# A Flamingo-style block on one core: new step orders in cross- and local attention, layer norms on ScalarE, roots taken in pairs, the queries' root inside the exponential

## What is computed

```python
def local_layer(x, wqkv, qs, ksc, wo, lg, lb, w1, b1, w2, b2):
    h = shift_token(x)
    q, k, v = split_heads(h @ wqkv)           # 8 heads of 64
    q, k = l2norm(q) * qs, l2norm(k) * ksc
    q, k = rotary_xpos(q, k)
    o = local_attention(q, k, v)              # windows of 64, each sees itself and the one before; softmax
    x = x + merge(o) @ wo
    h = layernorm(shift_token(x)) * lg + lb
    a, g = split(h @ w1 + b1)
    return x + (a * gelu(g)) @ w2 + b2

x = x + tanh(g_xattn[0]) * cross_attention_0(layernorm(x), ctx)   # 16 heads of 8, causal and padding mask
y = layernorm(x)
for l in range(2):
    y = local_layer(y, ...)
x = x + tanh(g_ffn[0]) * y
x = x + tanh(g_xattn[1]) * cross_attention_1(layernorm(x), ctx)   # with biases, padding mask
x = x + tanh(g_ffn[1]) * experts(layernorm(x))                    # 8 experts, the top two of a sigmoid router
```

## Time and profile before

| | |
|---|---|
| median of the runs | 1339.03 us |
| the profiled execution | 1336.5 us, its span 1334.6 us |
| mean granted TensorE clock | 0.969 |
| busy: TensorE, VectorE, ScalarE, GpSimd | 1147.0, 1070.7, 875.5, 876.7 us (86%, 80%, 66%, 66%) |
| chain that ended last | VectorE 33%, TensorE 25%, ScalarE 19%, issue 14%, GpSimd 6% |

### The profile page before, as it was taken

The page is one execution under the profiler, slowest core; times in us unless marked ns, Lnnn a source line. Parts: engine busy times, 40 slices in busy tenths (PEclk is TensorE's granted clock), DMA queues, the critical chain, the costliest instruction groups (busy, mean ns, idle before and its releaser), DMA issues.

```text
span 1334.6 us, 33990 instructions
## 1 busy us (share of the span) xinstructions
PE 1147.0 (86%) x11792; PEld 963.0 (72%) x11792; DVE 1070.7 (80%) x2430; ACT 875.5 (66%) x2445; POOL 876.7 (66%) x1060
## 2 busy tenths in 40 slices
PE   5487776689999997896899999979979999999997
PEld 3266654477777776895677777769966777899997
DVE  2799997788888884777888888858889998588887
ACT  1376664477877775454777777765557777666664
POOL 0567773999999993336999999953366664334442
PEclk8699998899999998997999999999989999999999
DMA  6100000000000000210011100001100000000000
GB/s 171 51 8 4 1 1 7 8 8 10 10 10 10 14 2 9 62 31 11 10 24 41 28 10 15 2 4 29 28 1 2 1 2 1 5 14 13 13 11 15
DMA packets 59418, 23.35 MB, mean 17 GB/s; under 512 B 49093, under 2 KB 57202, under 8 KB 59250
## 3 DMA queue, kind: packets, MB, share of 16 engines
q1 hardware_dynamic: 55296, 19.22, 6.0%
q10 hardware_dynamic: 3954, 1.96, 0.6%
HBM read 10.68 MB, written 2.10 MB: 10 GB/s over the span
## 4 chain that ended last, share of the span: by engine, by line
DVE 33%; PE 25%; ACT 19%; issue 14%; POOL 6%; ACTq 1%; DMA 1%; SPq 1%; DVEq 0%; POOLq 0%
ACT a_e L889 12%; PE m_ps_h L1232 7%; PE m_ps_y L1244 6%; DVE a_rot L994 6%; DVE x_e L626 6%; DVE x_stat L623 5%; DVE a_rot L996 3%; DVE a_stat L952 3%; ACT a_sq L896 2%; PE a_ps_t L804 2%; ACT x_qhh L532 2%; DVE a_stat L945 2%; PE f_ps_y L1089 1%; PE f_ps_g L1100 1%; POOL a_stat L1020 1%
## 5 line engine op out<-in xcount | busy, mean ns | idle before, releaser
L1020 POOL TENSOR_TENSOR a_stat<-a_stat,small 128x16 f32<-128x16 f32 x64 | 187.7, 2933 | 5.3
L889 ACT ACTIVATE a_e<-a_ps_s,a_stat 128x128 f32<-128x128 f32 x512 | 180.2, 379 | 4.4 <-DVE a_stat L952 3.5
L1030 POOL TENSOR_TENSOR a_e<-a_e,a_stat 128x1024 f32<-128x1024 f32 x64 | 121.4, 1896 | 19.6 <-DVE a_stat L981 19.6
L1024 POOL TENSOR_TENSOR a_rot<-a_rot,a_stat 128x1024 f32<-128x1024 f32 x64 | 121.8, 1903 | 5.0
L518 ACT ACTIVATE x_e<-x_e 128x1024 f32<-128x1024 f32 x64 | 67.8, 1060 | 69.9 <-DVE x_e L626 69.9
L889 ACT ACTIVATION_READ_ACCUMULATOR a_e<-a_ps_s,a_stat 128x1 f32 x512 | 111.4, 218 | 0.0
L994 DVE TENSOR_TENSOR a_rot<-a_ps_qk,a_rtab 128x512 f32<-128x512 f32 x128 | 87.9, 686 | 26.9 <-ACT a_sq L896 26.8
L882 ACT ACTIVATE a_eT<-a_ps_t 128x1024 f32<-128x1024 f32 x64 | 65.6, 1024 | 61.9 <-PE a_ps_t L804 59.3
L1130 ACT ACTIVATE f_gl<-f_ps_g,vec 128x128 f32<-128x128 f32 (+1 forms) x192 | 55.9, 361 | 64.1 <-PE f_ps_g L1100 64.1
L1016 POOL TENSOR_TENSOR a_rot<-a_rot 128x512 f32<-128x512 f32 x64 | 82.1, 1283 | 23.0 <-DVE a_rot L996 20.9
L1232 PE MATMUL m_ps_h<-m_hT,w 128*128 128x128 f32 x768 | 93.6, 278 | 0.0
(11 more groups left out here) (165 smaller groups left out, 3659.7 us busy)
## 6 DMA issues: line engine op xcount, KB each, us to landing
a_h<-y SPq DMA_DIRECT2D x64, 32.0 KB
f_h<-y SPq DMA_DIRECT2D x64, 32.0 KB
out_dram<-x SPq DMA_DIRECT2D x32, 64.0 KB, 1.5
a_h<-y SPq DMA_DIRECT2D x64, 31.8 KB
f_h<-y SPq DMA_DIRECT2D x64, 31.8 KB
wqkv<-in_L_ffn_wqkv_dram SPq DMA_DIRECT2D x2, 768.0 KB, 4.9
w<-in_L_ffn_w_dram SPq DMA_DIRECT2D x2, 768.0 KB, 5.5
c_ctx2T<-in_ctxT_dram SPq DMA_DIRECT2D x2, 512.0 KB, 3.2
```

The source lines that it names most:

```text
L889: act.activation(self.e[n % 2][:, P * i:P * i + P], ps_s[:, P * i:P * i + P], ACT.Exp, bias=stat[:, i:i + 1], accum_out=stat[:, 8 + i:9 + ...
L1020: p.tensor_tensor(t[:, 48:64], t[:, 32:48], g.neg_half.broadcast_to([P, 16]), ALU.pow).then_inc(self.s_n, 1)
L1024: p.tensor_tensor(r, r, t[:, 48:64].unsqueeze(2).broadcast_to([P, 16, LD]), ALU.mult).then_inc(self.s_n, 1)
L1030: p.tensor_tensor(e3, e3, self.stat[n % 2][:, 16:24].unsqueeze(2).broadcast_to([P, 8, P]), ALU.mult)\
```

## The change

- **Local attention, the roots.** Keys are still multiplied by their root on GpSimd (512 columns); the queries are not. Their root goes in as the `scale` of the exponential, and the maximum is multiplied by it on VectorE (8 columns). The mask is smaller in size (-1e24) for that. The statistics have four buffers where they had two.
- **Local attention, the order.** All engines have new sequences with lower depths. TensorE: transposes of e (s-6), v (s-4), h (s), o (s-6), transposes of q and k (s-2), qk (s, k first), y (s-6), scores (s-3). ScalarE: square q (s-1), kTr (s-3), copies of v (s-4, half of it to `vx` in each tile), eT (s-6), hT (s), exponentials (s-4), square k (s). The rounding of the weights (ScalarE) and the position tables (VectorE) move to step -3, the rest of the rounding to step -2, the loads to two steps earlier.
- **Cross-attention, the norms.** The `Norm` helper is no longer used. The statistics of the norm before the attention and (in cross 0) of the norm behind it, eight tiles earlier (`LAG`), are put side by side; GpSimd adds, takes one power of both and computes -mean * root (`roots`). ScalarE applies scale and bias for h and for y.
- **Cross-attention, the order.** New sequences and lower depths on all engines; on VectorE: subtraction (s-4), reciprocal (s-6), update of x (s-7), division (s-6), statistics (s), in cross 0 statistics for y (s-7), maximum (s-3), rest of the queries' rounding (s-2). The spread of the keys is divided between the two steps of a pair.
- **Starts.** 0, 36, 69, 106, 139, 174 and 209, and the steps begin at -3.

The core of the diff:

```diff
@@ Cross.scalar
+        n = s - 1
+        if 0 <= n < T:
+            k, t = T * l + n, self.st[n % 4]
+            act.wait_ge(self.s_rs, self.rooted(l, n))
+            after(act, self.s_h, k - 1)
+            act.activation(self.h[n % 2][:, :], tok(g.x, n), ACT.Identity, bias=t[:, 20:21], scale=t[:, 18:19]).then_inc(self.s_hn, 1)
+        m = n - LAG
+        if not l and 0 <= m < T:
+            t = self.st[n % 4]
+            act.wait_ge(self.s_rs, self.rooted(0, n))
+            act.activation(tok(g.y, m), tok(g.x, m), ACT.Identity, bias=t[:, 21:22], scale=t[:, 19:20]).then_inc(self.s_yn, 1)
@@ Cross.roots
+        p.tensor_scalar(t[:, 16 + lo:16 + hi], both[:, lo:hi, 1], 1e-5, None, ALU.add).then_inc(self.s_rs, 1)
+        p.wait_ge(self.s_rs, k + 1)
+        p.tensor_tensor(t[:, 18 + lo:18 + hi], t[:, 16 + lo:16 + hi], self.g.neg_half.broadcast_to([P, hi - lo]), ALU.pow)\
+            .then_inc(self.s_rs, 1)
+        p.wait_ge(self.s_rs, k + 2)
+        for i in range(lo, hi):
+            m = p.tensor_scalar(t[:, 20 + i:21 + i], t[:, 12 + 2 * i:13 + 2 * i], t[:, 18 + i:19 + i], -1.0, ALU.mult, ALU.mult)
@@ Local.tensor
+        n = s - 6
+        if 0 <= n < T:
+            k = T * l + n
+            pe.wait_ge(self.s_en, k + 1)
+            pe.wait_ge(self.s_qc, min(k + 4, end))
+            pe.wait_ge(self.s_kc, min(k + 4, end))
+            for i in range(2 * LP):
+                m = pe.transpose(ps_t[:, P * i:P * i + P], self.e[n % 2][:, P * i:P * i + P], g.ident)
+            m.then_inc(self.s_et, 1)
+        n = s - 4
+        if 0 <= n < T:
+            k = T * l + n
+            after(pe, self.s_vc, k)
+            after(pe, self.s_oc, k - 2)
+            self.project_h(pe, ps_b[:, :], n, 1024).then_inc(self.s_v, 1)
+        n = s
+        if 0 <= n < T:
...
+            pe.transpose(ps_a[:, 0:P], self.h[n % UNROLL][:, :], g.ident).then_inc(self.s_h, 1)
+        n = s - 6
+        if 0 <= n < T:
+            k, u, b = T * l + n, n % 2, n // 2
+            pe.wait_ge(self.s_ec, k + 1)
+            if u:
+                pe.wait_ge(self.s_vx[0], k // 2 + 1)
+                pe.wait_ge(self.s_vx[1], k // 2 + 1)
+            pe.wait_ge(self.s_vc, min(k + 3, end))
...
+                        m = pe.matmul(ps_b[LD * e:LD * e + LD, P * pair + WIN * x:P * pair + WIN * x + WIN],
@@ Local.scalar
+        n = s - 4
+        if 0 <= n < T:
+            k, u, b = T * l + n, n % 2, n // 2
+            rows = slice(0, WIN) if u else slice(WIN, P)
+            act.wait_ge(self.s_v, k + 1)
+            after(act, self.s_o, k - 2)
+            act.activation(self.vx[b % 2][rows, :], ps_b[rows, :], ACT.Copy).then_inc(self.s_vx[u], 1)
+            act.activation(self.vt[n % UNROLL][:, :], ps_b[:, :], ACT.Copy).then_inc(self.s_vc, 1)
+        n = s - 6
+        if 0 <= n < T:
+            k = T * l + n
+            act.wait_ge(self.s_et, k + 1)
+            after(act, self.s_o, k - 1)
+            act.activation(self.eT[n % 2][:, :], ps_t[:, :], ACT.Copy).then_inc(self.s_ec, 1)
...
+            for i in range(2 * LP):
+                e, pair = divmod(i, LP)
+                root = 48 + 2 * pair + e
+                act.activation(self.e[n % 2][:, P * i:P * i + P], ps_s[:, P * i:P * i + P], ACT.Exp, bias=stat[:, 24 + i:25 + i],
+                               scale=stat[:, root:root + 1], accum_out=stat[:, 8 + i:9 + i]).then_inc(self.s_e, 1)
@@ Local.gpsimd
+            r = self.rot[n % 2][:, INNER:].rearrange("p (h d) -> p h d", d=LD)
+            p.tensor_tensor(r, r, t[:, 56:64].unsqueeze(2).broadcast_to([P, LH, LD]), ALU.mult).then_inc(self.s_n, 1)
@@ build
-        for stage, l, later in ((cross, 0, 0), (local, 0, T + 4), (mlp, 0, T + 2), (local, 1, T + 4), (mlp, 1, T + 2),
-                                (cross, 1, T + 3), (experts, 0, T + 5)):
+        for stage, l, later in ((cross, 0, 0), (local, 0, T + 4), (mlp, 0, T + 1), (local, 1, T + 5), (mlp, 1, T + 1),
+                                (cross, 1, T + 3), (experts, 0, T + 3)):
```

More of the change, by code:

```diff
@@ L479, in tensor @@
             m.then_inc(self.s_s, 1)
-        n = s - 8
+        n = s - 2
+        if 0 <= n < T:
+            k = T * l + n
+            pe.wait_ge(self.s_hc, k + 1)
+            after(pe, self.s_qc, k)
+            after(pe, self.s_qr, k)
+            if n == 0 and l:
+                self.take(pe, l, "q")
+            for i in range(2):
+                m = pe.matmul(ps_q[:, P * i:P * i + P], g.wq[l][:, P * i:P * i + P], self.hT[n % 2][:, :], start=True, stop=True)
+            m.then_inc(self.s_q, 1)
+        n = s - 6
         if 0 <= n < T:
@@ L726, in sync @@
     def sync(self, sp, l, s):
-        if s == 0 and not l:
+        if s == -2 and not l:
             sp.wait_ge(self.s_z, 2)
-        n = s
+        n = s + 2
         if 0 <= n < T:
@@ new lines, in tensor @@
+        n = s - 2
+        if 0 <= n < T:
+            k = T * l + n
+            pe.wait_ge(self.s_n, 4 * k + 4)
+            pe.wait_ge(self.s_nq, k + 1)
+            after(pe, self.s_ec, k - 3)
+            after(pe, self.s_qc, k)
+            after(pe, self.s_kc, k)
+            if n == 0:
+                self.take(pe, l, "t")
+            for i in range(2 * LP):
+                m = pe.transpose(ps_t[:, P * i:P * i + P], self.rot[n % 2][:, P * i:P * i + P], g.ident)
+            m.then_inc(self.s_t, 1)
@@ new lines, in tensor @@
+        n = s
+        if 0 <= n < T:
+            k = T * l + n
+            pe.wait_ge(self.s_hc, k + 1)
+            pe.wait_ge(self.s_hr, k + 1)
+            if n == 0:
+                self.take(pe, l, "qk")
+            for i in range(2):
+                lo = INNER * (1 - i)
+                after(pe, self.s_sq, 2 * (k - 1) + i + 1)
+                after(pe, self.s_r, 4 * (k - 1) + 2 * i + 2)
+                self.project_h(pe, ps_qk[:, lo:lo + INNER], n, lo).then_inc(self.s_qk, 1)
+        n = s - 6
@@ new lines, in tensor @@
+        if 0 <= n < T:
+            k = T * l + n
+            pe.wait_ge(self.s_oc, k + 1)
+            after(pe, self.s_yc, k)
+            pe.wait_ge(self.s_hc, min(k + 7, end))
+            pe.wait_ge(self.s_hr, min(k + 7, end))
+            for pair in range(LP):
+                m = pe.matmul(ps_a[:, 0:D], self.oT[n % 2][:, P * pair:P * pair + P], g.lwo[:, D * pair:D * pair + D],
+                              start=(pair == 0), stop=(pair == LP - 1))
+            m.then_inc(self.s_y, 1)
```

517 lines of the change are left out of this document (229 added, 288 removed).

## The result

The changed kernel takes 1423.57 us (median of four runs, 1422.02 to 1425.22) against 1338.82 for the kernel before, a ratio of 1.063 [1.0616, 1.0645]. The forecast was 1371 with 1345 to 1405 as its range: the sign was right, 84.7 us were lost where 32.5 had been expected, and the time lies outside the range. The profiled execution has a span of 1420.8 us against 1334.6, so 86.2 us have to be found.

A forecast was written before the change was run, and what follows sets the result against it. GpSimd was taken to bound local attention, VectorE the first cross-attention, TensorE nearly the second. 1336.5 + 68 (local) - 20 - 6 (cross) - 9.5 (seams) = 1369.0, with 2.5 for the median 1371.5, stated as 1371 us; range 1345 to 1405.

The forecast's parts named there:

- one chain through TensorE and ScalarE: Local attention: transposes of e, v, ScalarE's copies, o, then TensorE's remaining groups in order, 9.8 us a step.
- some 2.1: Local attention: microseconds of each step in which TensorE stands empty, waiting in front of o for ScalarE's copies.
- 29 x 9.8 + 2 x 7.8: Local layer, 31 steps from tile 0's maximum to tile 31's: 299.8 us against 265.7, so +34 us.
- a rival at 0.08: Local attention: TensorE's clock falls, one step in ten at the lower clock, 37 us more, 1408 us; chance 0.08.
- 68 for both layers: Local attention: loss of 34 us in each of two layers, +68 us together, bounds +50 to +91.
- The seams: Passages between stages: -9.5 us together, bounds +5 to -22.
- I take 7 off: Seam between first cross-attention and first local maximum: 7 us less than its 33.7 us, with weight rounding moved earlier.
- -20: First cross-attention: 20 us gained as both norms leave VectorE for ScalarE, bounds 0 to -30.
- -6: Second cross-attention: 6 us gained as VectorE saves 9 us and TensorE caps it, bounds +3 to -12.
- why the step is no shorter: Local attention before: GpSimd's queue, 8.50 us from root to root without a gap that matters, sets the 8.57 us step.
- My rival of a faster kernel at 1262: Local attention: the detour through ScalarE doesn't bind, steps of about 7.9 us, each layer 21 us less; chance 0.09.
- 62 x 0.72 = 45 us: Local attention: the exponentials' second per-partition operand on ScalarE, 0.72 us a step, 45 us without cover, costed at nothing.

The follow-up runs named there:

- e1: Changed kernel with local v projection (tile s-3) moved to the end of TensorE's step, behind the scores: 1343.68 us, ratio 1.0024.
- e3: Changed kernel with 14 unused transposes of the identity in TensorE's queue ahead of h in local attention: 1401.76 us, ratio 1.0463.
- e9: Changed kernel with v last, scores a step later between transposes of e and h, padding row last, maximum ahead of k's rotation: 1385.47 us, ratio 1.0334.
- e7: Changed kernel with the rounding of weights and the position tables back at step 0 of both local stages: 1429.5 us, ratio 1.0687.
- e4: Kernel before with the changed kernel's cross-attention alone, experts two steps earlier, local attention as before: 1315.02 us, ratio 0.9812.
- e12: e5 with the changed kernel's early rounding (steps -3 and -2) in both local stages: 1303.29 us, ratio 0.9726.
- e2: Changed kernel with ScalarE's copy of e's transposes ahead of its two copies of v: 1360.52 us, ratio 1.0149.
- e5: e4 with ScalarE's copy of the padding row moved to the end of its cross-attention step: 1306.2 us, ratio 0.9766.
- e8: e4 with the queries' root moved from GpSimd into the exponential's scale, the maximum multiplied on VectorE: 1366.42 us, ratio 1.0204.
- e11: e8 without the exponentials' per-partition scale and with the unmultiplied maximum as bias: 1316.47 us, ratio 0.9822.
- e10: Changed kernel with v last, scores a step later between transposes of e and h, padding row last, maximum behind k's rotation: 1352.69 us, ratio 1.0114.

## Why the prediction was right and wrong

**Right: where the loss sits and how it works.** The forecast for a local step was 9.8 us by adding up one chain through TensorE and ScalarE; the steps at full clock are 9.72 and 9.87, the hole is 1.96 and 2.11 us where "some 2.1" stood, ended by the copy that was named. e1 shortens it by 0.9 us by moving one block. e3, with the clock held up, has 301.8 and 302.8 us for the 299.8 of the sum.

**The step that failed: "29 x 9.8 + 2 x 7.8" took the clock as 1.00.** I had its fall as a rival at 0.08, with one step in ten at the lower clock. It happened to 17 of 62, each for about 1.5 us rather than the 5.9 I gave it, 23.3 us by e3. With the clock held, e3 takes 1401.8 us, inside my range of 1345 to 1405. My argument against it was a comparison of busy shares in the earlier trace rows, and it is a bad one: a share over 100 us says nothing of how the idle time is divided. The kernel before has TensorE idle for 21.6 of those 100 us of cross 0, a larger share than the 38.6 of 200 here, and its clock is 1.00; its longest hole there is 1.44 us:

```profile
152.69 0.47 PE L477 MATMUL x_ps_s<-x_khl,x_qhh 128*128 128x512 f32 x1 [1.44 <-DVE x_e L626]
```

In e9 the steady step is as long, 9.80 us, but TensorE's idle time in it comes in pieces of 0.31, 0.47 and 0.66 us, 1.4 together, and the clock stays at 1.00. I had set the mechanism aside because no row showed it, and should have given it the weight of one that the change creates anew. The Trainium skill (TensorE: Matmul & The Clock Gate, HAM oscillation) describes a wait in every iteration that is paid for again and again in clock. This case's trace agrees in kind.

**The term "68 for both layers"** was 99.8. Besides the 23.3 of the clock, 3.3 come from giving layer 1 the 265.7 us of layer 0, where its own starts in the trace of before give 262.4, and 5.0 from first and last steps that I priced too low (9.73 and 9.77 on average in e3 where the sum had 9.67; some 2 of these 5.0 may be e3's own, as said there).

**The seams: -9.5 forecast, +7.5 measured, a miss of 17 us.** The term "I take 7 off" at the first seam failed: that seam is 1.9 us longer. The early rounding was worth 5.9 us in e7, but only 1.1 of it falls on cross 0 and this seam together; 4.9 lie between the local layers, where I had given it nothing. What I had left out is a queue effect between stages. In the last steps of cross 0 its norms for y, now on ScalarE, wait for a root from GpSimd, and GpSimd has the local roots ahead of it. The chain of waits of the changed kernel, over one such step:

```profile
202.52 1.23 DVE a_stat L1001
...
204.20 0.80 POOL a_stat L1081
...
207.09 1.28 POOL a_rot L1083
...
208.78 0.58 POOL x_st L669
...
209.76 0.02 ACT y L535
...
210.41 0.50 ACT a_sq L924
...
210.93 1.23 DVE a_stat L1001
```

From sum to sum are 8.4 us: the local root, the addition of k, then cross-attention's own small root (L669, L673), then y on ScalarE, and queued behind it the square from which the next sum comes. TensorE meanwhile idles; over 200 to 220 us it is 10.6 us busy, at a clock of 0.66. Before, VectorE did this norm. The norms on ScalarE alone don't cost this: e4 has them with the old local order, and its seam is 33.0 us for the 33.7 of before. The seam between cross 0 and the first local maximum is 35.6 us in the changed kernel, while e12, with the new cross-attention and rounding but the old local order, has 28.9. The new local order has its first sum sooner, 9.6 us after the last subtraction against 14.3, but then three more sums, 8.3 us each, stand before the first maximum, where e12 has two, 13.5 us together. This is read from the traces: no run takes the wait for GpSimd out of the new order, so how much of the 6.7 us it carries stays open.

Between the local layers 118.2 us pass where there were 114.4 before. e1, e2 and e3, with the same starts and without the falls of the clock, have 114.6, 114.2 and 114.8, which points to the lower clock; how it divides was not tried.

**Cross-attention.** Cross 0 was -19.2 for -20, with the 2.6 us of the early rounding in it. Cross 1 was -1.9 for -6, within its bounds; the term that was mis-sized is ScalarE's, where a copy of one partition that costs 1.06 us came to stand in front of the exponential in every second step (before, it stood behind). e5 shows it: moved away, cross 1 gains 6.7 us. My prediction hadn't mentioned it.

**Wrong without harm: that GpSimd's queue shows "why the step is no shorter".** The earlier trace rows show it without a gap, and I took that for the cause. e8 and e11 refute it: with GpSimd relieved the step doesn't shrink, and with the exponentials lengthened it grows by just their length. The chain of waits of the kernel before would have shown it. My rival of a faster kernel at 1262 rested in part on that reading, and so its 0.09 was too high. It did no harm because the new order hid ring and pointer both. In the old order the same part of the change, costed at nothing, costs 51 us: the sentence on its cover ("62 x 0.72 = 45 us" without it) was the right size.

## What to carry to other kernels

A queue that is full to 96% isn't proved to be the bound: follow the chain of waits from one step to the next, and look for a ring of the same length through other engines before pricing what an offloaded instruction gains. In a software pipeline, never issue a group whose result another engine must move right in front of the group that needs that move; the place of v cost 80 us here, the clock included. When a change puts one unbroken hole of about 2 us into each of TensorE's steps, count the clock in; fill the hole or break it up.

## What was not expected of the hardware

- **Short holes that recur lower TensorE's clock.** With a hole of 1.96 or 2.11 us in each step of 9.8 us, every third or fourth is followed by about 3 us at half the clock, 1.5 us lost each time. With holes of 1.35 and 1.63 us (e2, steps of 9.12 and 9.40), 1.09 and 1.24 us (e1) or several of at most 0.66 us (e9, steps of 9.80) the clock stayed at 1.00. Where between 1.63 and 1.96 it begins was not tried. Whether the longest hole or the idle time of a whole step decides isn't settled either: a step has 2.0 us of it in the changed kernel, 1.5 in e2 and 1.4 in e9.
- **Work without a use can pay.** In e3 transposes of a constant, 14 a step, held the clock at 1.00 and made the kernel 22 us faster.
- **A copy of one partition isn't cheap**: 1 x 1024 elements took ScalarE 1.06 us, as long as an exponential over 128 x 1024 in the same chain (1.07).
- **VectorE and GpSimd slow each other on SBUF operands.** VectorE's addition of q's halves (128x512, both inputs in SBUF) took 0.68 us in e8, beside GpSimd's root of 16 columns, and 1.68 in e10, beside its product of e. GpSimd's own product of k (128x512) took 1.04 us in e8 and 1.49 in e10. In e10 this whole microsecond lies off the chain of waits; in e9, where the addition takes 1.86 us, it lies on it. It wasn't tested by itself. The Trainium skill (GPSIMD Engine Reference, Specifications) says that the two share SBUF interfaces, with contention where VectorE has two SBUF inputs. These rows agree with it.
